# First steps of the convolution stage in another order: head 0's own work first, set-up inside head 0's steps

## The chip, the cores and the metric

One Trainium2 chip; the kernel runs on one of its cores. The metric is the time of one execution on the device in microseconds (us). An execution uses five instruction queues that run beside each other, each in its own order: PE (the matrix engine, TensorE), DVE (VectorE), ACT (ScalarE), POOL (GpSimd) and SP (which here only issues transfers). Semaphores let one wait for another.

## The reference

The kernel computes four blocks with residual sums: a long convolution between `x` and a context, a mixture-of-experts block, an attention block and a feed-forward block. Only the first one, and the preparation of the second that runs beside it, matter here:

```python
x = x + conv(layernorm(x), k, bias, ctx, ctx)      # first block
def conv(v, k, bias, x1, x2):                      # B=16, D=256, L=512, 8 rows to a head, 32 heads
    vr, x1r, x2r = (a.reshape(B, 32, 8, L) for a in (v, x1, x2))
    kv = vr[:, :, :, None, :] * x2r[:, :, None, :, :]
    y = causal_convolution(kv, k)                  # each head has one filter of 512 taps
    y = y + kv * bias.reshape(32, 8)[None, :, :, None, None]   # the skip term
    return einsum('bhijl,bhil->bhjl', y, x1r)
```

## The kernel before

`front_phase` is the first of three phases. It loops over 32 heads `h`; a head has two halves `u` and four steps `lb`. A half holds 4 product tiles of 128x512 (positions on the partitions). For each, `product` (POOL) multiplies the transposed rows `vt` with the turned context `ct` into `kf`. For the first two of a half, `parts` (ACT, `kh`) and `lows` (DVE for even, POOL for odd, `kl`) split it into a rounded part and a remainder. `conv` (PE) sums them against the filter's Toeplitz blocks: three matmuls per pair for `th`, `tl`, and one in full precision with their sum `t0` for the rest. A half takes 24 matmuls, 3 in its step 0, 9 up to its step 1, and the result of each step goes to one of four banks `Y`. DVE multiplies it with the context (`z`) and sums it (`R`).

Around this every head needs: `load` (SP: rows `x`, context `cr`, turned context `ct`, filter), `stats`, `shift` and `norm` (the layer norm: DVE, one exponentiation on POOL, DVE, ACT `xn`), `turn` (four PE transposes, an ACT copy to `vt`), `filt` and `filt_lo` (the filter through PE into `th`, `tl`, then `t0` on POOL), `weigh`, `skips` and `residual` (the skip term: DVE `w`, a PE matmul with the block of ones, DVE `sk`, POOL sum). The filters of heads 0 and 1 come straight from `k`; those of later heads from a table `kpad` in device memory that `split_filters` makes once: load `k`, round it (ACT, L108), residue (DVE, L109), store both (POOL, L293). `setup` (L419 on) loads what the next block needs, `gw`, `b1s`, `rb` and the bias table `f0b` (73x512), converts the last (ACT and DVE, `f_br`), and fills small constants on POOL. `clear` zeroes parts of a buffer `xs` from a tile of zeros. `shared_weights` takes one of eight 128x512 pieces of the shared weights: it converts the piece loaded one head before (ACT copy, POOL remainder, `c_sw`) and loads the next. `logit` and `best` handle the expert choice from head 2 on.

Each engine's queue is filled in the order in which the Python code calls these helpers. A wait is put down with the helper that needs it, so an engine that waits in one holds up everything queued behind it. In before, `load(0)`, `load(1)` and all of head 0's preparation, `split_filters` and `setup` are called ahead of the first `product`; in every head `shared_weights` and, from head 2 on, `logit` are called in half 0, step 1.

Of the kernel before, what the change touches and what calls it, by code (L numbers as in the profile page):

```python
# [126 lines left out]
def front_phase(nc, ctx, d, before, xa, idx, gat, ident, mhalf, n_heads=NHC):  # L127
# [110 lines left out]
    c_ob = p.do("gpsimd", lambda e: e.memset(ones_b, 1.0))  # L238

    v3 = ones_b.rearrange("p (b j) -> p b j", j=8)  # L240
    c_ob = p.do("gpsimd", lambda e: e.affine_select(out=v3, in_=v3, compare_op=ALU.is_ge, fill=0.0, base=0,
                                                    pattern=[[-8, 16], [0, 8]], channel_multiplier=1), c_ob)
    c_ob = p.do("gpsimd", lambda e: e.affine_select(out=v3, in_=v3, compare_op=ALU.is_ge, fill=0.0, base=7,
                                                    pattern=[[8, 16], [0, 8]], channel_multiplier=-1), c_ob)
    c_anr = p.do("vector", lambda e: e.tensor_copy(antir, anti), c_an)
    dsk = p.dsem("sk")
    c_sk = p.dma("sync", dsk, lambda e: e.dma_start(skip[:, :], d["skipt"]))
# [6 lines left out]
    c_z = p.do("gpsimd", lambda e: e.memset(zero[:, :], 0.0))  # L254
# [13 lines left out]
    def load(h):  # L268
        s = h % 2
        T["x", h] = p.dma("sync", dx[h % 4], lambda e: e.dma_start(xt[:, h % 4, :], d["x"][:, 8 * h:8 * h + 8, :]),  # L270
                          g("out", h - 4), gu("xb", h - 4))
        T["cr", h] = p.dma("sync", dr[s], lambda e: e.dma_start(cr[:, s, :], d["ctx"][:, 8 * h:8 * h + 8, :]),
                           g("sx", h - 2), g("w", h - 2))
        T["ct", h] = p.dma("sync", dc[h % 3], lambda e: e.dma_start(ct[:, h % 3, :, :], d["ctxh"][h]), g("z", h - 3), g("kv", h - 3))

        if h < 2:
            base = d["k"][h, 1:2]
            ap = bass.AP(base.tensor, base.offset, [[1, 128], [1, 512]])
            T["tf", h] = p.dma("sync", dt_[s], lambda e: e.dma_start(tf[:, s, :], ap))
# [28 lines left out]
    def filt_lo(h):  # L308
        s = h % 2
        if h < 2:  # L310
            T["tl", h] = p.do("vector", lambda e: e.tensor_tensor(tl[:, s, :], PT[:, :], f32(th[:, s, :]), ALU.subtract), g("th", h), g("mm", h - 2))
        else:
            T["pt", h] = p.do("tensor", lambda e: e.matmul(PT[:, :], antir, tr[:, s, 1, :], start=True, stop=True), g("tf", h), g("th", h))
            T["tl", h] = p.do("scalar", lambda e: e.activation(tl[:, s, :], PT[:, :], ACT.Copy), g("pt", h), g("mm", h - 2))
        T["t0", h] = p.do("gpsimd", lambda e: e.tensor_tensor(t0[:, s, :], f32(th[:, s, 0:256]), f32(tl[:, s, 0:256]), ALU.add), g("th", h), g("tl", h), g("mm", h - 2))
# [398 lines left out]
    stats(1)  # L714
    shift(1)
    split_filters()
    setup()
    units = [(h, u, mb) for h in range(n_heads) for u in range(2) for mb in range(4)]
    for n in range(4):
        product(*units[n])  # L720
        parts(*units[n])
    product(*units[4])
    for h in range(n_heads):
        more = h + 1 < n_heads
        for u in range(2):
            for lb in range(4):
# [11 lines left out]
                if u == 0 and lb == 0 and more:  # L738
                    weigh(h + 1)
# [1035 lines left out]
```

How the kernel before makes its waits and increments, by code:

```python
    def emit(self, e, eng):  # L72
        seen = {}
        def wait(sem, v):
            if seen.get(id(sem), 0) < v:
                eng.wait_ge(sem, v)
                seen[id(sem)] = v
        for sem, v in self.before:
            wait(sem, v)
        for fn, waits, inc in self.q[e]:
            for w in waits:
                if w is not None:
                    wait(*w)
            ins = fn(eng) if fn else None
            if inc:
                ins.then_inc(*inc)
# [1665 lines left out]
                def run(eng, e=e):  # L1754
                    for p in phases:
                        p.emit(e, eng)
                    if e == "sync":
                        for sem, v in before:
                            eng.wait_ge(sem, v)
```

## Time and profile before

| what | value |
|---|---|
| median of 3 executions | 3274.34 us (3273.34 to 3274.57) |
| profiled execution | 3277.38 us |
| its span, first to last instruction | 3275.6 us |
| PE busy over the span | 3175.7 us (97%) |
| DVE, ACT, POOL busy | 2173.6, 1267.7, 1051.4 us |
| PE's mean granted clock | 0.99 of full speed |
| instructions | 51687 |

The profile is one execution. Its busy times say how long each engine had an instruction running, an average over three quite different phases; the convolution stage is about the first 620 us. Records of PE overlap since matmuls are pipelined, so the distance between the starts tells the pace. Names begin with `c_` or `f_` for tiles of this phase; a number at the end is left out.

### The profile page before, as it was taken

The page shows a single profiled execution, that of the slowest core. Times are in us where ns is not written, and L with a number is a line of the kernel's source. Part 1 is how long each engine was busy: PE and PEld are TensorE (multiplying, and loading weights), DVE is VectorE, ACT ScalarE, POOL GpSimd, SP SyncE. Part 2 cuts the span into 40 slices and gives each one's busy share as a digit, 9 for nine tenths or more (in the row PEclk, how much of TensorE's full clock was granted, in tenths as well). Part 3 has the DMA queues.
Part 4 walks back from the last instruction along what each step waited for, and adds up shares of the span by engine and source line. Part 5 has one row for each costly group of instructions (what it writes and reads, how often), then busy time and mean ns, then how long its engine had stood idle before and what let it go on. Part 6 is the DMA issues. An engine that isn't in the chain of part 4 may idle for free.

```text
span 3275.6 us, 51687 instructions
## 1 busy us (share of the span) xinstructions
PE 3175.7 (97%) x18581; PEld 2699.7 (82%) x18581; DVE 2173.6 (66%) x5817; ACT 1267.7 (39%) x3058; POOL 1051.4 (32%) x1111
## 2 busy tenths in 40 slices
PE   7999999999999889999999999999998999999999
PEld 4666666689899769999999999999997788888887
DVE  6888888756555577778878787777776533333332
ACT  2333333333344345555555555555554311111111
POOL 7877777535211122222222222222201011010110
PEclk9999999999999899999999999999999999999999
DMA  4544443259644521111111111111101300000000
GB/s 129 155 142 133 132 140 95 81 171 313 194 155 151 207 90 53 46 46 46 46 46 40 39 46 46 46 39 40 46 14 44 108 26 26 26 26 26 26 14 13
DMA packets 123780, 267.41 MB, mean 82 GB/s; under 512 B 17689, under 2 KB 18337, under 8 KB 123530
## 3 DMA queue, kind: packets, MB, share of 16 engines
q1 hardware_dynamic: 100122, 186.59, 18.2%
q0 software_dynamic: 23408, 77.51, 7.0%
q8 instruction: 153, 2.51, 0.3%
q14 instruction: 97, 0.79, 0.1%
HBM read 159.49 MB, written 104.56 MB: 81 GB/s over the span
## 4 chain that ended last, share of the span: by engine, by line
PE 79%; DVE 9%; POOL 7%; ACT 1%; DMA 1%; issue 1%; SPq 0%; POOLq 0%; DVEq 0%
PE g_PH L1046 11%; PE g_O L1069 11%; PE t_U L1511 10%; PE t_S L1463 9%; PE t_PO L1498 5%; PE t_M L1447 5%; POOL c_kf L358 3%; PE t_T L1485 3%; PE f_Y L920 3%; PE f_Y L691 3%; PE t_M L1402 2%; PE f_Y L385 2%; PE f_Y L390 2%; DVE c_R L403 2%; DVE c_z L397 2%; PE t_M L1384 2%
## 5 line engine op out<-in xcount | busy, mean ns | idle before, releaser
L1473 ACT ACTIVATE t_pr<-t_sm,t_nb 128x256 f32<-128x256 f32 x512 | 256.5, 502 | 368.5 <-DVE t_nb L1469 368.5
L1059 DVE CAST g_hh<-g_hf 128x512 fp32r<-128x512 f32 x128 | 61.8, 483 | 434.7 <-PE g_O L1069 429.9
L1417 POOL TENSOR_TENSOR t_r<-t_r 128x256 f32<-128x256 f32 x128 | 95.9, 750 | 778.9 <-DVE t_rw L1479 451.7
L358 POOL TENSOR_TENSOR c_kf<-c_vt,c_ct 128x512 f32<-128x512 f32 x256 | 296.6, 1179 | 0.0
L1058 ACT ACTIVATE g_hf<-g_PH,g_b1s 128x512 f32<-128x512 f32 x128 | 88.2, 689 | 519.1 <-PE g_PH L1046 519.1
L1480 DVE TENSOR_SCALAR t_pr<-t_pr,t_rw 128x256 f32<-128x256 f32 x512 | 222.0, 434 | 18.2
L390 PE MATMUL f_Y<-c_kh,c_th 128*128 128x512 f32 x448 | 199.9, 446 | 9.6 <-ACT c_kh L365 9.6
L1046 PE MATMUL g_PH<-g_xh,g_w1h 128*128 128x512 f32 x512 | 205.3, 401 | 1.5 <-DVE g_xl L1034 1.5
L1046 PE MATMUL g_PH<-g_xh,g_w1l 128*128 128x512 f32 x512 | 203.0, 396 | 0.0
L1046 PE MATMUL g_PH<-g_xl,g_w1h 128*128 128x512 f32 x512 | 202.6, 396 | 0.0
L1069 PE MATMUL g_O<-g_w2h,g_hh 128*128 128x512 f32 x512 | 202.3, 395 | 0.0
L1069 PE MATMUL g_O<-g_w2h,g_hl 128*128 128x512 f32 x512 | 202.1, 395 | 0.0
L1511 PE MATMUL t_U<-t_voh,t_oth 128*128 128x512 f32 x512 | 201.7, 394 | 0.0
L1511 PE MATMUL t_U<-t_voh,t_otl 128*128 128x512 f32 x512 | 201.7, 394 | 0.0
L1069 PE MATMUL g_O<-g_w2l,g_hh 128*128 128x512 f32 x512 | 201.5, 394 | 0.0
L1469 DVE CUSTOM_DVE_ANT_0 t_sm<-t_S,t_mk 128x256 f32<-128x256 f32 x512 | 194.8, 418 | 9.6 <-PE t_S L1463 9.6
L1511 PE MATMUL t_U<-t_vol,t_oth 128*128 128x512 f32 x512 | 200.8, 392 | 0.0
L397 DVE TENSOR_TENSOR c_z<-f_Y,c_ct 128x512 f32<-128x512 f32 x256 | 174.1, 680 | 33.2 <-PE f_Y L385 32.9
L1490 DVE TENSOR_TENSOR t_ptl<-t_T,t_pth 128x512 fp32r<-128x512 f32 x256 | 175.6, 686 | 15.1 <-ACT t_pth L1489 15.0
L385 PE MATMUL f_Y<-c_kf,c_t 128*128 128x512 f32 x384 | 185.4, 591 | 0.0
L403 DVE TENSOR_REDUCE c_R<-c_z 128x64 f32<-128x512 f32 x256 | 174.9, 683 | 6.7
L390 PE MATMUL f_Y<-c_kl,c_th 128*128 128x512 f32 x448 | 177.8, 397 | 0.0
(356 smaller groups left out, 9696.1 us busy)
## 6 DMA issues: line engine op xcount, KB each, us to landing
xs<-c_zero SPq DMA_DIRECT2D x71, 256.0 KB, 5.2
f_xg<-xs SPq DMA_DIRECT2D x71, 256.0 KB, 2.8
ys<-f_yt POOLq DMA_DIRECT2D x71, 256.0 KB, 2.4
c_tr<-kpad SPq DMA_DIRECT2D x60, 256.0 KB, 4.8
f_xg<-xn SPq DMA_DIRECT2D x40, 256.0 KB, 4.6
c_xt<-x SPq DMA_DIRECT2D x32, 256.0 KB, 3.5
c_cr<-ctx SPq DMA_DIRECT2D x32, 256.0 KB, 3.9
c_ct<-ctxh SPq DMA_DIRECT2D x32, 256.0 KB, 4.4
```

What stands on the lines that cost most here:

```text
L358: T["kv", h] = T["kv1", n] = p.do("gpsimd", lambda e: e.tensor_tensor(o, iv, ic, ALU.mult), g("vt", h), g("ct", h), g("kl", n - 8), g("kh" ...
L385: last = p.do("tensor", lambda e, c=c, mb=mb: e.matmul(Y[y % 4][:, :], t0[:, s, c], kf[:, v, mb, :], start=False, stop=mb == lb), g("t0", ...
L390: last = p.do("tensor", lambda e, a=a, b_=b_, c=c, mb=mb, i=i: e.matmul(Y[y % 4][:, :], a[:, s, c], b_[:, v, mb, :], start=(mb == 0 and i ...
L397: T["z", h] = T["z1", y] = p.do("vector", lambda e: e.tensor_tensor(zz.rearrange("p (b j i) -> p b j i", i=8, j=8), iv, ic, ALU.mult), las ...
L403: T["red", y] = T["R", h] = p.do("vector", lambda e: e.tensor_reduce(rr, zr, AXX, ALU.add), g("z1", y), g("pr", h - 2))
L1046: T["ph", n] = p.do("tensor", lambda e, kk=kk, a=a, b_=b_, i=i: e.matmul(ph[:, :], a[:, k, kk, :], b_[:, s, kk, :], start=i == 0, stop=i = ...
L1069: tk = p.do("tensor", lambda e, a=a, b_=b_, t=t, fin=fin, c=c, beg=beg: e.matmul(O[t][:, :], a[:, n % 2, c], b_[:, k, :], start=beg, stop= ...
L1463: a = p.do("tensor", lambda e, t=t, j=j, q=q, k=k: e.matmul(PS1[:, 256 * t:256 * t + 256], q, k[:, s, :], start=j == 0, stop=j == 4), g("q ...
L1469: T["am", N] = am = p.do("vector", lambda e, t=t, k4=k4: e.tensor_tensor_reduce(out=sm[:, k4, :], in0=PS1[:, 256 * t:256 * t + 256], in1=m ...
L1473: T["ex", x] = p.do("scalar", lambda e, t=t, k4=k4: e.activation(pr[:, N % 2, t, :], sm[:, k4, :], ACT.Exp, bias=nb[:, k4, 0:1], scale=-1. ...
L1480: T["nm", x] = p.do("vector", lambda e, t=t, k4=k4: e.tensor_scalar(pr[:, N % 2, t, :], pr[:, N % 2, t, :], rw[:, k4, 1:2], None, ALU.mult ...
L1511: a = p.do("tensor", lambda e, t=t, tt=tt, j=j, o=o, w=w: e.matmul(PU[t][:, :], o[:, N % 3, tt], w[:, h, :], start=h == 0 and j == 0, stop ...
```

## The change

Three things are done. First, `load` is cut into four parts, and head 0's rows, filter and turned context are issued ahead of the rest; head 0's normalisation, transposes, filter and its first product follow directly, and product 1 comes after the statistics of head 1. Second, what is left of the preparation moves between head 0's steps: `split_filters` and the block of ones behind step 0, the skip term and the tile of zeros behind step 1, its residual sum behind step 2 and `setup` behind step 3; the skip product of head 1 moves from step 0 to step 2. Third, `shared_weights` is called in half 1, step 0 of every head instead of half 0, step 1.

```diff
-    c_ob = p.do("gpsimd", lambda e: e.memset(ones_b, 1.0))
...
-    c_sk = p.dma("sync", dsk, lambda e: e.dma_start(skip[:, :], d["skipt"]))
...
-    c_z = p.do("gpsimd", lambda e: e.memset(zero[:, :], 0.0))
...
+    def block_ones():
+
+        c_ob = p.do("gpsimd", lambda e: e.memset(ones_b, 1.0))
...
+        U["ones",] = c_ob
...
+        if h:
+            sum_filter(h)
+
+    def sum_filter(h):
+        s = h % 2
         T["t0", h] = p.do("gpsimd", lambda e: e.tensor_tensor(t0[:, s, :], f32(th[:, s, 0:256]), f32(tl[:, s, 0:256]), ALU.add), g("th", h), g("tl", h), g("mm", h - 2))
...
-    load(0)
-    load(1)
+    load_rows(0)
+    load_filter(0)
+    load_turned(0)
+    load_rows(1)
+    load_context(0)
+    U["skip",] = p.dma("sync", dsk, lambda e: e.dma_start(skip[:, :], d["skipt"]))
+    load_turned(1)
+    load_context(1)
+    load_filter(1)
     stats(0)
+    shift(0)
+    norm(0)
+    turn(0)
     filt(0)
     filt_lo(0)
-    shift(0)
-    norm(0)
-    weigh(0)
-    turn(0)
-    skips(0)
-    residual(0)
+    units = [(h, u, mb) for h in range(n_heads) for u in range(2) for mb in range(4)]
+    product(*units[0])
+    parts(*units[0])
+    sum_filter(0)
     stats(1)
     shift(1)
-    split_filters()
-    setup()
-    units = [(h, u, mb) for h in range(n_heads) for u in range(2) for mb in range(4)]
-    for n in range(4):
+    for n in range(1, 4):
         product(*units[n])
         parts(*units[n])
     product(*units[4])
...
-                if u == 0 and lb == 0 and more:
+                if u == 0 and lb == (0 if h else 2) and more:
                     weigh(h + 1)
...
                 conv(h, u, lb, units[n] if n < len(units) and lb == 0 else None)
                 if u == 0 and lb == 3 and h:
                     finish(h - 1)
+                if h == 0 and u == 0:
+                    if lb == 0:
+                        split_filters()
+                        block_ones()
+                    if lb == 1:
+                        weigh(0)
+                        skips(0)
+                        U["zero",] = p.do("gpsimd", lambda e: e.memset(zero[:, :], 0.0))
+                    if lb == 2:
+                        residual(0)
+                    if lb == 3:
+                        setup()
...
-                if u == 0 and lb == 1:
+                if u == 1 and lb == 0:
                     shared_weights()
-                    if h > 1:
-                        logit(h - 2)
+                if u == 0 and lb == 1 and h > 1:
+                    logit(h - 2)
```

POOL's queue from head 0's exponentiation (`c_rs`) on, before:

```order
L123 TENSOR_TENSOR c_rs<-c_rs,mhalf 128x1 [waits c_vector]
L315 TENSOR_TENSOR c_t<-c_th,c_tl 128x256 [waits c_vector,c_scalar]
L349 TENSOR_TENSOR c_sk<-c_sk,c_xt 128x512 [waits c_x0,c_vector]
L123 TENSOR_TENSOR c_rs<-c_rs,mhalf 128x1 [waits c_vector]
L293 DMA kpad<-f_xh 32x640 [waits c_vector,c_scalar]
L293 DMA kpad<-f_xl 32x640
L428 MEMSET f_gt 128x146
L430 MEMSET f_gt 128x2 [waits c_gpsimd]
L430 MEMSET f_gt 128x2 x2
L431 MEMSET c_onef 128x128
L433 AFFINE_SELECT c_trif<-c_onef 128x128 [waits c_gpsimd]
L436 IOTA c_iota 128x8
```

And in the changed kernel, from the same place:

```order
L123 TENSOR_TENSOR c_rs<-c_rs,mhalf 128x1 [waits c_vector]
L378 TENSOR_TENSOR c_kf<-c_vt,c_ct 128x512 [waits c_c0,c_scalar]
L335 TENSOR_TENSOR c_t<-c_th,c_tl 128x256 [waits c_vector,c_scalar]
L123 TENSOR_TENSOR c_rs<-c_rs,mhalf 128x1 [waits c_vector]
L378 TENSOR_TENSOR c_kf<-c_vt,c_ct 128x512
L393 TENSOR_TENSOR c_kl<-c_kf,c_kh 128x512 [waits c_gpsimd,c_scalar]
L378 TENSOR_TENSOR c_kf<-c_vt,c_ct 128x512 x4
L308 DMA kpad<-f_xh 32x640 [waits c_vector,c_scalar]
L308 DMA kpad<-f_xl 32x640
L292 MEMSET c_ones_b 128x128
L295 AFFINE_SELECT c_ones_b<-c_ones_b 128x128 [waits c_gpsimd]
L297 AFFINE_SELECT c_ones_b<-c_ones_b 128x128 [waits c_gpsimd]
```

The two stores of the filter table and the block of ones (`c_ones_b`, which stood ahead of all this) now come behind six products, and the small fills of `setup` have left this place.

SP's queue from head 1's filter on, before:

```order
L279 DMA f_xg<-k 128x512
L289 DMA f_xg<-k 32x640
L421 DMA c_gw<-gw 128x32
L422 DMA f_b1s<-sb 128x4
L423 DMA c_rb<-rb 8x256
L424 DMA f_stg<-f0b 73x512
L447 DMA f_stg<-sw 128x512
L270 DMA c_xt<-x 128x1x512
L272 DMA c_cr<-ctx 128x1x512 [waits c_vector]
L274 DMA c_ct<-ctxh 128x512
L284 DMA c_tr<-kpad 128x512 [waits c_tensor,c_ko]
L284 DMA c_tr<-kpad 128x512
```

And in the changed kernel:

```order
L259 DMA c_xt<-x 128x1x512
L264 DMA c_cr<-ctx 128x1x512 [waits c_vector]
L268 DMA c_ct<-ctxh 128x512
L280 DMA c_tr<-kpad 128x512 [waits c_tensor,c_ko]
L280 DMA c_tr<-kpad 128x512
L252 DMA xs<-c_zero 128x512 [waits c_gpsimd]
L252 DMA xs<-c_zero 128x512 x2
L441 DMA c_gw<-gw 128x32
L442 DMA f_b1s<-sb 128x4
L443 DMA c_rb<-rb 8x256
L444 DMA f_stg<-f0b 73x512
L467 DMA f_stg<-sw 128x512
```

The four loads of `setup` (`gw`, `sb`, `rb`, `f0b`) stood ahead of head 2's rows; they now stand behind head 2's context, which waits for DVE (`c_vector`, the skip term of head 0), behind the filter loads from `kpad` and behind three clears.

ACT's queue from the first product's rounded part on, before (its first row is the table's rounding):

```order
L108 ACTIVATE f_xh<-f_xg 32x640 [waits c_kp]
L426 ACTIVATE f_br<-f_stg 73x512 [waits c_uc0]
L365 ACTIVATE c_kh<-c_kf 128x512 [waits c_gpsimd] x2
L323 ACTIVATE c_xn<-c_xt,c_nm,c_rs 128x512 [waits c_x1,c_vector]
L365 ACTIVATE c_kh<-c_kf 128x512 [waits c_gpsimd] x2
L337 ACTIVATE c_vt<-f_PV 128x512 [waits c_tensor]
L306 ACTIVATE c_th<-f_PT 128x512 [waits c_tensor]
L365 ACTIVATE c_kh<-c_kf 128x512 [waits c_gpsimd] x2
```

And in the changed kernel:

```order
L385 ACTIVATE c_kh<-c_kf 128x512 [waits c_gpsimd] x2
L343 ACTIVATE c_xn<-c_xt,c_nm,c_rs 128x512 [waits c_x1,c_vector]
L385 ACTIVATE c_kh<-c_kf 128x512 [waits c_gpsimd]
L108 ACTIVATE f_xh<-f_xg 32x640 [waits c_kp]
L385 ACTIVATE c_kh<-c_kf 128x512 [waits c_gpsimd]
L357 ACTIVATE c_vt<-f_PV 128x512 [waits c_tensor]
L446 ACTIVATE f_br<-f_stg 73x512 [waits c_uc0]
L321 ACTIVATE c_th<-f_PT 128x512 [waits c_tensor]
L385 ACTIVATE c_kh<-c_kf 128x512 [waits c_gpsimd] x2
```

The conversion of the bias table (`f_br`, which waits for the transfers `c_uc0`) stood ahead of all copies of products; it now stands ahead of head 1's filter copy `c_th` and of the copies of head 1's first two products.

## Rows read from the trace of the kernel before

**Rows 1.** windows: time, length, then busy us (instructions) per engine, PE clock, DMA share, GB/s

```profile
16.00:17.00 1.00, 0.46 (x1) 0.00 (x0) 0.50 (x1) 0.00 (x0) 0.00 (x0) 1.00 0.06 25
26.00:30.00 4.00, 3.90 (x10) 3.11 (x11) 1.76 (x2) 0.77 (x2) 3.85 (x4) 1.00 1.03 335
61.97:81.42 19.45, 18.51 (x79) 12.91 (x78) 16.67 (x32) 6.91 (x12) 15.90 (x16) 1.00 0.52 149
238.27:257.22 18.95, 18.67 (x79) 12.91 (x78) 16.62 (x33) 6.28 (x11) 14.66 (x15) 1.00 0.44 140
```

**Rows 2.** timeline of PE: start us, us, engine, line, op, names; in brackets the idle time before

```profile
26.10 0.77 PE L390 MATMUL f_Y<-c_kh,c_th 128*128 128x512 f32 x1 [9.64 <-ACT c_kh L365]
...
44.52 0.79 PE L390 MATMUL f_Y<-c_kh,c_th 128*128 128x512 f32 x1
```

**Rows 3.** chain that ended last, 0 to 60 us: start us, us, what

```profile
12.67 0.82 ACT c_xn L323
...
13.54 1.12 PE f_PV L335 x4
14.65 1.82 PE f_PSK L342 x2
...
19.22 0.80 DVE f_xl L109
...
20.63 1.22 POOL kpad L293 x2
...
23.34 2.08 POOL c_kf L358 x2
...
32.78 1.40 PE f_Y L390 x6
```

**Rows 4.** timeline of POOL in the first 34 us

```profile
2.38 0.41 POOL L241 TENSOR_SCALAR_AFFINE_SELECT c_ones_b<-c_ones_b 128x128 f32<-128x128 f32 x1
...
5.92 0.56 POOL L123 TENSOR_TENSOR c_rs<-c_rs,mhalf 128x1 f32<-128x1 f32 x1 [2.19 <-DVE c_rs L122]
...
26.14 1.28 POOL L373 TENSOR_TENSOR c_kl<-c_kf,c_kh 128x512 fp32r<-128x512 f32 x1 [0.74 <-ACT c_kh L365]
27.38 6.08 POOL L358 TENSOR_TENSOR c_kf<-c_vt,c_ct 128x512 f32<-128x512 f32 x5
```

**Rows 5.** timeline of ACT (ScalarE), 0 to 82 us

```profile
11.19 0.60 ACT L306 ACTIVATE c_th<-f_PT 128x512 fp32r<-128x512 f32 x1 [9.10 <-PE f_PT L303]
...
18.98 0.63 ACT L426 ACTIVATE f_br<-f_stg 73x512 fp32r<-73x512 f32 x1 [3.08 <-DMA f_stg<-f0b]
...
30.98 0.63 ACT L365 ACTIVATE c_kh<-c_kf 128x512 fp32r<-128x512 f32 x1 [4.21 <-POOL c_kf L358]
...
68.56 0.16 ACT L499 ACTIVATE c_lg<-f_PV 128x8 f32<-128x8 f32 x1
```

**Rows 6.** timeline of SP's DMA issues, 0 to 30 us

```profile
6.68 0.47 SPq L421 DMA_DIRECT2D c_gw<-gw  x1
...
8.22 0.24 SPq L424 DMA_DIRECT2D f_stg<-f0b  x1
...
17.21 0.54 SPq L272 DMA_DIRECT2D c_cr<-ctx  x1
...
23.41 0.81 SPq L284 DMA_DIRECT2D c_tr<-kpad  x2
24.26 1.45 SPq L262 DMA_DIRECT2D xs<-c_zero  x3
```

**Rows 7.** timeline of DVE, 26 to 48 us

```profile
37.49 0.69 DVE L397 TENSOR_TENSOR c_z<-f_Y,c_ct 128x512 f32<-128x512 f32 x1
...
41.78 0.69 DVE L120 BATCH_NORM_STATS2 c_st<-c_xt 128x6 f32<-128x512 f32 x1
...
42.79 0.68 DVE L311 TENSOR_TENSOR c_tl<-f_PT,c_th 128x512 fp32r<-128x512 f32 x1
```

**Rows 8.** source line L262, the three clears at 24 to 26 us

```profile
DMA to landing us min/median/max: 4.3/4.5/5.0
```

More of the change, by code:

```diff
@@ L261, in clear @@
         for c in left[:n]:
-            U["clr",] = p.dma("sync", dz, lambda e, c=c: e.dma_start(xsz[:, c:c + 512], zero[:, :]), c_z)
+            U["clr",] = p.dma("sync", dz, lambda e, c=c: e.dma_start(xsz[:, c:c + 512], zero[:, :]), U["zero",])
         del left[:n]
@@ L266, in g, with load_rows, load_context, load_turned @@
         return T.get(k)
-    def load(h):
-        s = h % 2
+    def load_rows(h):
         T["x", h] = p.dma("sync", dx[h % 4], lambda e: e.dma_start(xt[:, h % 4, :], d["x"][:, 8 * h:8 * h + 8, :]),
                           g("out", h - 4), gu("xb", h - 4))
+    def load_context(h):
+        s = h % 2
         T["cr", h] = p.dma("sync", dr[s], lambda e: e.dma_start(cr[:, s, :], d["ctx"][:, 8 * h:8 * h + 8, :]),
                            g("sx", h - 2), g("w", h - 2))
+    def load_turned(h):
         T["ct", h] = p.dma("sync", dc[h % 3], lambda e: e.dma_start(ct[:, h % 3, :, :], d["ctxh"][h]), g("z", h - 3), g("kv", h - 3))
+    def load_filter(h):
+        s = h % 2
         if h < 2:
@@ L284, in load @@
                 T["tf", h] = p.dma("sync", dt_[s], lambda e, q=q, ap=ap: e.dma_start(f32(tr[:, s, q, :]), ap), T["kp",], g("pt", h - 2))
+    def load(h):
+        load_rows(h)
+        load_context(h)
+        load_turned(h)
+        load_filter(h)
+    dsk = p.dsem("sk")
+    def block_ones():
+        c_ob = p.do("gpsimd", lambda e: e.memset(ones_b, 1.0))
+        v3 = ones_b.rearrange("p (b j) -> p b j", j=8)
+        c_ob = p.do("gpsimd", lambda e: e.affine_select(out=v3, in_=v3, compare_op=ALU.is_ge, fill=0.0, base=0,
+                                                        pattern=[[-8, 16], [0, 8]], channel_multiplier=1), c_ob)
+        c_ob = p.do("gpsimd", lambda e: e.affine_select(out=v3, in_=v3, compare_op=ALU.is_ge, fill=0.0, base=7,
+                                                        pattern=[[8, 16], [0, 8]], channel_multiplier=-1), c_ob)
+        U["ones",] = c_ob
     def split_filters():
@@ L314, in filt_lo @@
             T["tl", h] = p.do("scalar", lambda e: e.activation(tl[:, s, :], PT[:, :], ACT.Copy), g("pt", h), g("mm", h - 2))
+        if h:
+            sum_filter(h)
+    def sum_filter(h):
+        s = h % 2
         T["t0", h] = p.do("gpsimd", lambda e: e.tensor_tensor(t0[:, s, :], f32(th[:, s, 0:256]), f32(tl[:, s, 0:256]), ALU.add), g("th", h), g("tl", h), g("mm", h - 2))
@@ L329, in weigh @@
                                                                    in1=cr[:, s, :], op0=ALU.mult, op1=ALU.mult),
-                         g("xn", h), c_sk, g("cr", h), g("psk", h - 2))
+                         g("xn", h), U["skip",], g("cr", h), g("psk", h - 2))
     def turn(h):
@@ L342, in skips @@
         T["psk", h] = p.do("tensor", lambda e: e.matmul(PSK[:, :], ones_b, w[:, s, :], start=True, stop=True),
-                           c_ob, g("w", h), g("sx", h - 1))
+                           U["ones",], g("w", h), g("sx", h - 1))
         a = p.do("vector", lambda e: e.tensor_tensor(sk[:, s, :], cr[:, s, :], PSK[:, :], ALU.mult), g("psk", h), g("out2", h - 2))
```

6 lines of the change are left out of this document (removed).

## The prediction

> **What bounds the kernel now.** I read the windows first, then the chain that ended last, then the timelines of the engines over the first 48 us. The windows of two whole heads [rows 1] show a period of 19.45 us in an early head and 18.95 us in a later one, with PE busy for more than 17.7 of them in both, DVE for 16.6 and POOL for 14.7 to 15.9: this stage runs at the pace of PE with DVE close behind, and POOL has slack. So nothing that only moves work off POOL is worth anything in mid-stage. What counts is when the regular rhythm starts, and what the two periods differ by. The rhythm starts late: PE sits idle for 9.64 us before the first convolution matmul at 26.10 [rows 2]. The chain before it [rows 3] is the whole set-up in a row: normalise 12.67, transposes 13.54, the skip term's matmul 14.65, the filter table's residue 19.22, its two stores 20.63, and only then the first products at 23.34. The reader is to see that little of this feeds a convolution, so that there is something to win. The question is where the displaced work queues up.
>
> **The part that gets earlier.** Head 0's exponentiation on POOL stood at 5.92 [rows 4]. The rows' load moves up one issue, worth the 0.47 to 0.54 us that an issue takes [rows 6]: I take 0.45, which gives 5.5 to 6.0, the normalised rows at 6.3, transposes at 7.2 and their copy at 8.3 (0.87 and 1.15 later, as 12.67, 13.54 and that one's 1.12 [rows 3]). The first product runs from 9.0 to 10.0 (2.08 for two [rows 3]). The filter's matmul queues on PE behind the transposes: 8.3 to 10.4, its copy to 11.0 (0.60 [rows 5]), its residue to 11.7 (0.68 [rows 7]). POOL's second exponentiation now stands ahead of product 1. It waits for DVE's statistics of head 1, which stand behind the filter residue and the first low part: 12.6, 1.0 us of statistics (41.78 to 42.79 [rows 7]), 0.4 of hand-overs and 0.56 on POOL: 14.5. Product 1 ends at 15.6; the low part starts 0.7 later and takes 1.28 [rows 4]: 17.6, against 27.4 before. **This is a lead of 9.8 us, and the first convolution is ready at 12.7.**
>
> **Where the lead goes.** On PE the skip matmul now stands right behind the second convolution step, and it needs the block of ones. On POOL these three instructions stand behind four products and the two stores of the filter table, and the stores wait for DVE's residue, behind low part 4. Product 4 to its copy: 27.38 to 30.98 is 3.6 [rows 4, 5], so 21.2. Copy 0.63, low part and a reduction 1.5 (0.68 to 0.88 for such a DVE instruction), residue 0.80 [rows 3]: 24.1. The stores begin 0.6 after it and take 1.22 [rows 3]: 25.9. The ones: longest of three 0.41 [rows 4], I take 1.2 together: 27.2. The skip matmul there lasts 2.0 (14.65 to 16.5 and a start [rows 3]), the second convolution step having ended long ago: 29.2. In before PE stood at this very step, nine matmuls on, near 29.9: from 26 to 30 only ten ran, so 0.43 us apart after 26.10, and later six in 1.40 us, 0.23 each [rows 1 to 3]. After its new pause from about 20 to 27 PE runs so slowly again, 3.4 more matmuls at 0.2 us each, and the lead of 0.7 is used up: it ends the third step at 32.2 as before. (A slow start of this kind, nine matmuls at 0.2 more, costs 1.7 us; after a pause of 7 us rather than 9.6 it is assumed, so 0 to 1.7.) **Value of the earlier start for PE: 0 (bounds: 0, and the 9.8 if PE never waited).**
>
> A rule says why those matmuls are slow. The Trainium skill (TensorE: Matmul & The Clock Gate, "Part 1: The HAM clock gate") says that an idle PE falls back to half its clock and is released by activity. The spacing of 0.43 and 0.23 agrees, the granted clock of 1.00, the 2.4 GHz level, in the window of 26 to 30 [rows 1] does not. By the rule every restart after such a pause is slow, by the granted clock none is; the two differ by those 1.7 us.
>
> **The part that gets later.** This decides it. SP's second row load waits for the skip term's DVE product: 17.21 before [rows 6], now 29.2 + 0.7 = 29.9. Behind it on SP stand, in this order, the turned context, two filter loads, three clears, and then set-up's four loads, which in before were issued from 6.68 to 8.22. From 17.21 the first two take 1.2, the filter loads 0.85, the clears 1.5, the three small ones 1.54 [rows 6]: the bias load (f0b) is issued at 35.05 instead of 8.22. The third clear (issued near 33) lands 4.3 to 5.0 after issue [rows 8], at 37.3 to 38.5, the longer with two more 256 KB loads ahead. The bias load is odd: 73 partitions, 146 KB. In the window 16 to 17 the queue carries 25 GB/s at a DMA share of 0.06, one sixteenth [rows 1], with nothing else pending, and ACT waits 3.08 us until 18.98 for exactly this load [rows 5]. I read this as one of 16 engines carrying it alone: 149.5 kB at 25 GB/s is 6.0 us. So it lands at 43.3 to 44.5; I take 43.7.
>
> That reading has a rule behind it. The Trainium skill (DMA: Bandwidth & Descriptors, "Why a DMA increments its semaphore by 16 and not by 1") says that a transfer goes over the largest number of engines up to 16 that divides its slowest dimension; 73 is prime, so one. The trickle agrees.
>
> On ACT the conversion of this load (f_br) now stands behind head 0's transposed copy and **ahead of head 1's filter copy** and of the copies of products 8 and 9. All wait until 43.75. On DVE the residue of f_br and three small casts stand ahead of z4: 0.4 after ACT starts, 0.68 and some 0.7 for the casts: z4 at 45.6 to 45.8, 37.49 before. From z4 to head 1's filter residue 5.30 us passed [rows 7], of which some 0.2 was waiting: that residue starts at 50.9 instead of 42.79, **8.1 us late**. POOL's filter sum and head 1's first convolution wait for it. PE runs on through its eighth step to about 44.6 (it has four output banks), then waits to 51.6 for head 1's first matmul, which began at 44.52 before [rows 2]: 7.1 late, and 8.8 if it restarts slowly. DVE and POOL are 8.1 late and pace head 1 as much as PE does. **I take 8.4 (bounds 7.1 and 8.8 for this landing time; 5.5 to 10 with it).**
>
> **The shared weights.** Their conversion moves from step 1 to step 4 of each head. At its old place ACT does it between product 9's copy and the logit copy: the logit copy comes at 68.56 [rows 5], and PE's transposes behind it wait for the bank. The two windows [rows 1] differ in just this pair, ACT 6.91 against 6.28 busy and POOL 15.90 against 14.66, and by 0.50 to 0.52 us in length. Heads 2 to 8 have both a logit and a conversion: 7 x 0.51 = 3.6 us. At the new place POOL comes to the exponentiation, where it waits for DVE (2.19 us even in head 0 [rows 4]), and it has 18.95 - 14.66 = 4.3 us idle in a later head, ACT 12.7 [rows 1]; so the 1.2 us are hidden there and count 0. If that cover is gone it costs what it did, 3.6. **Term: -3.6 (bounds -3.6 and 0.)**
>
> Set-up's POOL work (1.4 us), the zero fill and the residual sum move into head 0's steps. POOL has then not caught up on its old place and is still 1 to 2 us ahead, and later waits for the filter sum anyway: 0. The filter loads of head 2 come 8 us later and are used half a head after head 1 begins, which is itself late: 0.
>
> **Sum:** 0 + 8.4 - 3.6 = +4.8 us. The profiled execution of before took 3277.38 (span 3275.6, 1.8 around it), 3.0 above the median of 3274.34; it would give 3282.2, and the median 3279.1.
>
> **Rivals.**
> - *The bias load is no straggler, or lands ahead of the clears.* For it: it is small. Against: the 25 GB/s. It would land 4.5 us after its issue, as the clears do [rows 8]: ACT is free at 39.6, 4.1 earlier, so 8.4 becomes 4.3, sum +0.7: 3275.0. Chance 0.17. If it stalls nobody, -3.6: 3270.7, chance 0.08.
> - *The shared conversion costs the same at its new place* (ACT would do it between the copies of products 12 and 13). For it: ACT is in order and product 13's copy comes 0.5 later. Against: that copy is needed a step later. Sum +8.4, 3282.7: slower by 0.26%. It decides from 1.8 us of the 3.6 lost. Chance 0.15.
> - *The lead is kept*: the ones and the bias load turn out early and POOL's 9.8 us carry through. For it: the rows of start-up. Against: the order of POOL and SP. -9.8 - 3.6: 3260.9, the one case that is faster. Chance 0.05.
> - *The change does nothing*: excluded as a mechanism, since the order differs, but 3275 is close to it.
>
> **How the numbers follow.** The forecast has 0.55, its own range 3276 to 3281. A measurement of this kernel tells about 0.2%, 6.5 us, from no change, so the forecast and the first rival in both its forms count as no change: 0.80; slower 0.15, faster 0.05. The range reaches to the case without a stall and to the one with the conversion's price: 3270.7 to 3282.8. It leaves out the kept lead and what lies above.
>
> **What would show it.** In the profile after: the first product near 9, the first convolution matmul near 12.7; PE idle from about 20 to 27 and again from 44.6 to 51.6; ACT waiting some 10 us before f_br for f_stg<-f0b, until 43.7; head 1's filter residue at 50.9 and its sum on POOL near 51.7; and 18.95 between the filter sums of heads 3 to 9. It is wrong if f_br starts before 40, or if the periods stay at 19.45.

## The result and the profile after

Before and after were timed on one chip in turn: 3274.77 us before (3273.34 to 3280.19, 6 runs) and 3285.61 us after (3284.84 to 3287.93, 6 runs), a ratio of 1.003 with a 95% interval of 1.002 to 1.0041. The change makes the kernel 0.3% slower, 10.8 us by the medians. The forecast of 3279.1 was too low, and the result lies 2.8 us above the range. The profiled execution took 3286.95 us (span 3285.2), 9.6 more than that of before.

The loss can be placed to some tenths of a microsecond by a beacon, an instruction that runs once a period: here POOL's filter sum (`c_t`), once a head. First the timeline of POOL before, then after, the rows of the sums of heads 1, 2, 9 and 31:

```profile
43.55 0.73 POOL L315 TENSOR_TENSOR c_t<-c_th,c_tl 128x256 f32<-128x256 f32 x1
61.97 0.73 POOL L315 TENSOR_TENSOR c_t<-c_th,c_tl 128x256 f32<-128x256 f32 x1
...
198.23 0.73 POOL L315 TENSOR_TENSOR c_t<-c_th,c_tl 128x256 f32<-128x256 f32 x1
...
620.73 0.72 POOL L315 TENSOR_TENSOR c_t<-c_th,c_tl 128x256 f32<-128x256 f32 x1
```

```profile
45.77 1.26 POOL L393 TENSOR_TENSOR c_kl<-c_kf,c_kh 128x512 fp32r<-128x512 f32 x1 [8.67 <-ACT c_kh L385]
...
51.78 0.73 POOL L335 TENSOR_TENSOR c_t<-c_th,c_tl 128x256 f32<-128x256 f32 x1
72.14 0.74 POOL L335 TENSOR_TENSOR c_t<-c_th,c_tl 128x256 f32<-128x256 f32 x1
...
123.89 1.27 POOL L488 TENSOR_TENSOR c_sw<-f_stg,c_sw 128x512 fp32r<-128x512 f32 x1 [1.22 <-ACT c_sw L487]
...
209.34 0.74 POOL L335 TENSOR_TENSOR c_t<-c_th,c_tl 128x256 f32<-128x256 f32 x1
...
631.87 0.73 POOL L335 TENSOR_TENSOR c_t<-c_th,c_tl 128x256 f32<-128x256 f32 x1
```

The sum of head 1 is 8.23 us late, that of head 2 is 10.17 late, that of head 9 is 11.11 late, and that of head 31 is 11.14 late. So the whole loss arises in three places: 8.23 in start-up, 1.94 in head 1, and 0.94 in the seven periods from the sum of head 2 to that of head 9. The period, the distance of one head's sum from the next, was 19.47 there and is 19.60; from the sum of head 9 on both kernels have the same distances within 0.03, 18.95 in most heads. What follows the last sum takes 2654.9 us of the span before and 2653.3 after, and it scatters by a few us from one execution to the next: beacons compare parts, and medians compare kernels.

Start-up, in the chain that ended last of the kernel after (start, length, what):

```profile
25.33 0.41 POOL c_ones_b L297
...
32.21 1.30 SPq L441
33.55 1.09 SPq L442
...
34.68 0.38 SPq L443
...
35.11 8.41 DMA f_stg<-f0b
43.54 0.64 ACT f_br L446
44.20 0.68 DVE f_br L447
...
45.36 0.59 DVE c_z L417
45.95 1.63 DVE c_kl L393
...
51.10 0.61 DVE c_tl L326
...
51.80 6.45 PE f_Y L410 x15
```

The longest piece before head 1 is the bias load: issued at 35.11 instead of 8.22 [rows 6], it takes 8.41 us, and what follows in the chain, up to head 1's first matmul, starts from its landing. `c_tl`, the filter residue, is the last thing that this matmul waits for. On PE, the timeline shows the two pauses and what comes behind the second:

```profile
25.79 2.08 PE L362 MATMUL f_PSK<-c_w,c_ones_b 128*128 128x512 f32 x2 [7.28 <-POOL c_ones_b L297]
...
51.80 0.77 PE L410 MATMUL f_Y<-c_kh,c_th 128*128 128x512 f32 x1 [7.69 <-DVE c_tl L326]
52.36 0.63 PE L410 MATMUL f_Y<-c_kh,c_tl 128*128 128x512 f32 x1
52.79 0.63 PE L410 MATMUL f_Y<-c_kl,c_th 128*128 128x512 f32 x1
...
59.62 0.40 PE L410 MATMUL f_Y<-c_kh,c_tl 128*128 128x512 f32 x1
59.85 0.40 PE L410 MATMUL f_Y<-c_kl,c_th 128*128 128x512 f32 x1
```

```profile
50.00:52.00 2.00, 0.20 (x1) 0.23 (x2) 1.93 (x6) 0.00 (x0) 0.79 (x2) 0.50 0.27 42
52.00:54.00 2.00, 2.00 (x5) 1.59 (x6) 1.93 (x5) 0.82 (x1) 2.00 (x3) 0.50 0.27 97
54.00:56.00 2.00, 2.00 (x6) 1.54 (x5) 1.93 (x3) 0.00 (x0) 2.00 (x2) 0.50 0.46 145
56.00:58.00 2.00, 2.00 (x6) 1.57 (x6) 1.04 (x2) 1.26 (x2) 2.00 (x3) 0.56 0.84 154
58.00:62.00 4.00, 4.00 (x17) 2.51 (x16) 3.00 (x5) 0.60 (x1) 4.00 (x4) 1.00 0.72 248
```

The second fence holds windows of the kernel after, with the granted clock (the share of full speed that TensorE was allowed) third from the end. Behind the pause of 7.69 us matmuls start 0.43 apart at a granted clock of 0.50 (the 1.2 GHz level) and then 0.23 apart at 1.00 (2.4 GHz). The chain has 6.45 us for head 1's first fifteen.

The last place is mid-stage. The timeline of DVE, the low part of a filter product in head 4 and in head 12:

```profile
124.37 1.33 DVE L393 TENSOR_TENSOR c_kl<-c_kf,c_kh 128x512 fp32r<-128x512 f32 x1
...
281.35 0.68 DVE L393 TENSOR_TENSOR c_kl<-c_kf,c_kh 128x512 fp32r<-128x512 f32 x1
```

The same instruction takes 1.33 us in an early head and 0.68 in a later one. The early one overlaps the shared weights' remainder on POOL (`c_sw` at 123.89, above), which the change has put there. A second pair like it shows in start-up: POOL's low part at 45.77 (above) and DVE's at 45.95, which takes 1.63 in the chain.

### The profile page after: what moved, and what is told of

Read it like the earlier page. It is cut to its first block, busy times and chain, and to the rows that moved or that the text cites. A ratio compares the mean times of both kernels' runs of the same rounds, so it can differ in the third digit from the quotient of the medians.

```text
span 3285.2 us, 51684 instructions
## 1 busy us (share of the span) xinstructions
PE 3178.4 (97%) x18581; PEld 2700.9 (82%) x18581; DVE 2182.1 (66%) x5817; ACT 1267.4 (39%) x3058; POOL 1052.2 (32%) x1111
## 4 chain that ended last, share of the span: by engine, by line
PE 78%; DVE 10%; POOL 7%; ACT 1%; DMA 1%; issue 1%; SPq 0%; POOLq 0%; DVEq 0%
PE g_PH L1083 11%; PE g_O L1106 11%; PE t_U L1548 10%; PE t_S L1500 9%; PE t_PO L1535 5%; PE t_M L1484 5%; POOL c_kf L378 3%; PE t_T L1522 3%; PE f_Y L957 3%; PE f_Y L711 3%; PE t_M L1439 2%; DVE c_R L423 2%; PE f_Y L405 2%; PE f_Y L410 2%; DVE c_z L417 2%; PE t_M L1421 2%
```

## The experiments

All were timed in turn with the kernel before on their chip. The last three columns hold beacons: the filter sums of heads 1 and 2, the mean period from head 2 to head 9, and the sum of head 31. Two theories stood at the start: that the late bias load sets head 1 (A), and that POOL's remainder of the shared weights slows DVE's low part (D). Rivals were that something else late in start-up holds head 1 back, and that the conversion on ACT costs at its new place what it did at its old.

| run | median us (runs) | before, same chip | ratio, 95% | sums of heads 1, 2 | period | last sum |
|---|---|---|---|---|---|---|
| e1_loads_early | 3277.48 (11) | 3275.66 | 1.0008 [0.9999, 1.0017] | 44.95, 63.58 | 19.60 | 623.38 |
| e2_bias_split | 3279.14 (11) | 3275.66 | 1.0011 [1.0002, 1.002] | 46.92, 65.54 | 19.60 | 625.20 |
| e3_shared_old_place | 3282.97 (11) | 3275.66 | 1.0023 [1.0014, 1.0032] | 52.20, 70.85 | 19.47 | 629.66 |
| e4_before_logit_first | 3272.46 (11) | 3275.66 | 0.9991 [0.9982, 1.0] | 43.83, 62.19 | 18.95 | 617.40 |
| e5_ones_early | 3282.61 (10) | 3278.55 | 1.0013 [1.0004, 1.0022] | 47.14, 65.75 | 19.60 | 625.47 |
| e7_no_remainder | 3282.14 (10) | 3278.55 | 1.0011 [1.0001, 1.002] | 51.53, 70.22 | 18.95 | 625.54 |
| e8_loads_logit | 3276.9 (11) | 3278.55 | 0.999 [0.9981, 0.9999] | 44.28, 62.62 | 18.95 | 617.77 |
| e9_skip_late | 3275.67 (11) | 3278.55 | 0.9991 [0.9982, 1.0] | 45.14, 63.50 | 18.95 | 618.82 |
| e10_pe_awake | 3293.62 (5) | 3278.23 | 1.0045 [1.0032, 1.0059] | 52.10, 77.40 | 19.60 | 637.12 |
| e11_pe_awake_short | 3287.69 (8) | 3276.97 | 1.003 [1.0019, 1.004] | 51.39, 70.02 | 19.60 | 629.81 |

The beacon and the medians agree: the last sum's distance from 620.73 and the difference of the medians lie within 1.7 us of each other in every row. For e1 they are +2.7 and +1.8, for e4 -3.3 and -3.2, for e10 +16.4 and +15.4.

**e1_loads_early**: the changed kernel with set-up's four loads issued in head 0's first step.

```diff
-    def setup():
+    def setup_loads():
 
         p.dma("sync", dc0, lambda e: e.dma_start(gw[:, :, :], d["gw"]))
...
         nst[0] = 1
+
+    def setup():
+
...
                     if lb == 0:
                         split_filters()
+                        setup_loads()
                         block_ones()
```

> The changed kernel, but set-up's four loads are issued right behind the load of the filter table, in head 0's step 0; its arithmetic stays in step 3. Theory A (the bias load, late on SP and carried by one of 16 engines, holds up ACT and all of head 1): the conversion f_br follows head 0's copy at about 32.5, head 1's filter residue comes near 41.5 instead of 51.0, PE does not pause at 42.7, and the kernel gains 9 to 12 us on the changed one, to about 3275. Rival B (the start-up is late because of the skip matmul's wait for the block of ones, 18.1 to 25.8, and what POOL does behind it): nothing of that is touched, so under 2 us gained.

The last sum moves from 631.87 to 623.38, a gain of 8.49 us: a little under the 9 to 12 of theory A, and far from rival B's 2. PE's pause ahead of head 1 is gone; the rest of start-up stays. PE, and DVE's part:

```profile
44.98 0.47 PE L410 MATMUL f_Y<-c_kh,c_th 128*128 128x512 f32 x1 [0.39 <-issue]
```

```profile
36.87 1.25 DVE L450 TENSOR_TENSOR f_br<-f_stg,f_br 9x512 fp32r<-9x512 f32 x1
38.15 1.20 DVE L455 CAST c_one<-c_onef 128x128 fp32r<-128x128 f32 x1
...
44.20 0.68 DVE L326 TENSOR_TENSOR c_tl<-f_PT,c_th 128x512 fp32r<-128x512 f32 x1
```

Head 1's filter residue starts at 44.20, 2.7 later than expected: the conversion's residue and the first cast take 1.25 and 1.20, while they take 0.68 and 0.23 in the chain of after where POOL stands still. They run here beside POOL's products and its low part. These 1.54 us are about what is left of the delay: head 1's sum, at 44.95, is 1.40 later than in before.

**e2_bias_split**: the changed kernel with the bias load in two pieces; nothing is issued earlier.

```diff
-        U["c0",] = p.dma("sync", dc0, lambda e: e.dma_start(stg[0:73, 0, :], d["f0b2"]))
+        p.dma("sync", dc0, lambda e: e.dma_start(stg[0:64, 0, :], d["f0b2"][0:64]))
+        U["c0",] = p.dma("sync", dc0, lambda e: e.dma_start(stg[64:73, 0, :], d["f0b2"][64:73]))
```

> The changed kernel, but the 73-partition bias load is two loads, of 64 and of 9 partitions, at the same place. Theory A (one engine carries 73 partitions): both land about 4.5 us after their issue, f_br begins near 39.5 to 40 instead of 43.54, and everything from head 1 on is 3.5 to 4 us earlier; a gain of about 4 us. Rival C (the load is late only because of what is queued ahead of it, not because of its shape): f_br stays at 43 to 44 and the time at the changed kernel's.

The timeline of ACT:

```profile
38.67 0.63 ACT L447 ACTIVATE f_br<-f_stg 73x512 fp32r<-73x512 f32 x1 [5.59 <-DMA f_stg<-f0b]
```

The conversion starts 4.87 us earlier than the 43.54 of after, more than the 3.5 to 4 expected, the filter sum of head 1 is 4.86 earlier and the last sum 6.67. (The further 1.8 arise in head 1: PE's pause is only 2.18 us here, its granted clock stays at 1.00, and the sums of heads 1 and 2 lie 18.62 apart.) That shows two things: it is the shape of this load that makes it slow, since the bytes and the place in the queue are the same, and start-up hangs on it one for one. The Trainium skill (DMA: Bandwidth & Descriptors, "Why a DMA increments its semaphore by 16 and not by 1") has a load go over the largest number of engines up to sixteen that divides its slowest dimension: one for 73 partitions, sixteen for 64, nine for 9. For the 73 partitions the trace of after agrees: while nothing else is under way, its window shows 26 GB/s at a DMA share of 0.07, about one sixteenth.

```profile
39.00:43.00 4.00, 4.00 (x15) 2.64 (x14) 0.00 (x0) 0.00 (x0) 0.00 (x0) 1.00 0.07 26
```

How many engines carried the 64 and the 9 no run here shows; the 4.87 us fit.

**e3_shared_old_place** and **e4_before_logit_first** ask what the shared weights cost at either place.

```diff
e3, on the changed kernel:
-                if u == 1 and lb == 0:
+                if (u == 0 and lb == 1) if h else (u == 1 and lb == 0):
                     shared_weights()
e4, on the kernel before:
                 if u == 0 and lb == 1:
-                    shared_weights()
                     if h > 1:
                         logit(h - 2)
+                    shared_weights()
```

> The changed kernel, but the shared weights are converted in half 0, step 1 again (from head 1 on). Theory D (at the new place POOL's remainder runs beside DVE's low part, which then takes 1.33 instead of 0.68 us on the path, while at the old place ACT's copy delays the logit copy by 0.5): the distance between filter sums of heads 2 to 8 goes from 19.60 to 19.46, the low part of step 4 takes 0.68 again, about 1 us gained over seven heads and up to 0.7 in head 1. Rival E (the conversion is hidden at the new place and the periods are long for another reason of the new order): no change of the periods.

> The kernel before, with logit called ahead of shared_weights in half 0, step 1, nothing else. Theory D: ACT's logit copy no longer waits behind the 0.6 us conversion, and POOL's remainder stays where it runs beside DVE instructions that read PSUM; the periods of heads 2 to 8 fall from 19.46 to about 18.95, 3.6 us gained on before, near 3271. Rival E: POOL's 1.27 us cost something wherever they are and the periods stay above 19.3, under 1 us gained.

In e3, at the old place, the period is 19.47, as before, and DVE's low part takes 0.68 again; head 1 gains more than the 0.7 expected, 1.71 (18.65 for 20.36), which comes up again below. In e4, with the logit's copy ahead of the conversion, the period is 18.95. So the 0.51 per head was indeed the logit's copy waiting for the conversion on ACT, and the 3.6 us of the prediction are there to be had: e4 has its last sum 3.33 earlier than before. What the conversion costs at the new place they leave open.

**e7_no_remainder**: the changed kernel, with POOL's subtraction for the shared weights replaced by a memset of its result; it leaves out the low parts of the shared expert's weights.

```diff
-            U[key] = U["wl", i] = p.do("gpsimd", lambda e: e.tensor_tensor(to[1], src, f32(to[0]), ALU.subtract), U["wh", i], U["wd", i])
+            U[key] = U["wl", i] = p.do("gpsimd", lambda e: e.memset(f32(to[1]), 0.0), U["wh", i], U["wd", i])
```

> The changed kernel, but POOL's remainder of the shared weights is a fill with zeros instead of a subtraction with two operands (so the shared expert's result lacks its low parts). Theory D (the subtraction beside DVE's low part slows that one down): the low part of step 4 takes 0.68 instead of 1.33 us, the distance of the filter sums of heads 2 to 8 falls from 19.60 to 18.95, and the stage ends 4.5 to 5.5 us earlier than the changed kernel's. Rival H (ACT's copy, which delays product 13's copy, or the loads cost it): the periods stay at 19.5 or above.

POOL, then DVE, in head 4:

```profile
120.66 0.53 POOL L488 MEMSET c_sw<- 128x512 f32 x1 [1.20 <-ACT c_sw L487]
```

```profile
121.16 0.68 DVE L393 TENSOR_TENSOR c_kl<-c_kf,c_kh 128x512 fp32r<-128x512 f32 x1
```

The memset has all but ended when DVE's low part starts; this takes 0.68, and the period is 18.95. ACT's conversion is untouched. POOL's own length is not what counts: behind the subtraction of after it is idle for 2.22 us, until DVE hands it its next input. This isolates the cause: 0.65 us in each early head is DVE's low part waiting for POOL's subtraction. The last sum is 6.33 us earlier, more than the 4.5 to 5.5 expected, since head 1 is shorter too, by 1.67 (18.69 for 20.36). The Trainium skill (SBUF — State Buffer, "🔬 SBUF: two separate sides") says that a VectorE instruction in a two-port mode, or with two SBUF inputs beside a GpSimd one that reads SBUF, and the GpSimd instruction exclude each other for the whole instruction. The trace agrees: POOL's ends at 125.16 (123.89 and 1.27), and DVE's ends 0.54 later, at 125.70, as if it had begun only then. In e1 both slow instructions look alike: POOL's products end at 37.58 and DVE's residue at 38.12, POOL's low part ends at 39.27 and the cast at 39.35.

**e10_pe_awake** and **e11_pe_awake_short** ask what PE's slow restart has to do with head 1's 1.94 us: spare matmuls on PE in its pause, 60 and 23 of them (the cut shows e11).

```diff
+                if h == 1 and u == 0 and lb == 0:
+                    for _ in range(23):
+                        p.do("tensor", lambda e: e.matmul(Y[0][:, 0:128], ident, ident, start=True, stop=True), c_id, g("z1", 4), inc=False)
                 conv(h, u, lb, units[n] if n < len(units) and lb == 0 else None)
```

> The changed kernel with sixty spare 128 x 128 matmuls (identity by identity, 0.11 us each by the four transposes in 0.44 us, so some 6.6 us) put ahead of head 1's first convolution matmul on TensorE, into a bank that this matmul starts afresh. Nothing else is moved, and the bias load still holds head 1 back to a filter sum at 51.8. Theory that TensorE's slow restart after its pause is worth 1.7 us: the granted clock from 50 to 58 is 1.00, head 1's matmuls start 0.23 apart and not 0.43, the filter sums of heads 1 and 2 lie 18.6 us apart and not 20.36, the last filter sum is at 630.1 +- 0.3 and not at 631.87, and the time is about 3284 us. Rival, that VectorE and the shared weights' remainder set head 2's filter sum anyway: the matmuls are faster, the distance stays at 20.3 and the last filter sum at 631.9. Third: the clock falls or the restart is slow all the same, since the matmuls behind the pause are of another kind: spacing 0.43 and distance 20.3.

> As the run before it, with 23 spare matmuls in place of sixty: a float matmul of this size is two records of 0.112 us (13.66 us for 120), so 23 take 5.2 us, from 46.3, where their bank comes free, to 51.5. TensorE then pauses for 1.9 us and not for 7.7 ahead of them, and they are done when head 1's filter is. Theory that the slow restart is worth 1.7 us: granted clock 1.00 from 50 to 58, head 1's matmuls 0.23 apart from about 51.8, the filter sums of heads 1 and 2 18.6 apart and not 20.36, the last filter sum at 630.1, the time about 3284 us. Rival, that VectorE and the shared weights' remainder set head 2's filter sum anyway: the matmuls 0.23 apart, the distance 20.3, the last filter sum at 631.9 and the time as that of the changed kernel.

Sixty were too many: a float matmul of this size shows as two records, so they ran for 13.66 us, to 60.0, and held head 1's convolution back. The run says nothing on the distance of 20.36 (its own is 25.30), but head 1's matmuls started 0.23 apart right behind them. With 23 the pause is covered. Windows and PE's timeline of e11:

```profile
52.00:54.00 2.00, 2.00 (x10) 1.64 (x9) 1.97 (x5) 0.82 (x1) 2.00 (x3) 1.00 0.06 20
54.00:56.00 2.00, 2.00 (x9) 1.24 (x9) 1.55 (x3) 0.09 (x1) 2.00 (x3) 1.00 0.80 227
```

```profile
45.62 5.40 PE L776 MATMUL f_Y<-ident 128*128 128x128 f32 x46 [1.37 <-DVE c_z L417]
51.41 0.47 PE L410 MATMUL f_Y<-c_kh,c_th 128*128 128x512 f32 x1 [0.39 <-issue]
51.72 0.39 PE L410 MATMUL f_Y<-c_kh,c_tl 128*128 128x512 f32 x1
```

The granted clock stays at 1.00, the matmuls are 0.23 apart, and the filter sums of heads 1 and 2 lie 18.63 apart instead of 20.36, 1.73 less. (The last sum is 2.06 earlier; 0.39 of it is there at the sum of head 1 already.) The median does not resolve these 2 us: its ratio is 1.003, like that of the changed kernel.

Yet 1.73 is not the price of a slow restart alone. In e3 and e7 PE pauses for 8.63 and 8.30 us, the granted clock behind the pause is 0.50 and the matmuls start 0.43 apart, and still the two sums lie only 18.65 and 18.69 apart, where before has 18.42. What these two lack is POOL's subtraction in step 4 of head 1. From the chain of after, the chain of e3, and DVE's timeline of e11:

```profile
65.30 1.59 DVE c_kl L393
```

```profile
52.23 5.73 PE f_Y L410 x15
...
65.02 0.60 DVE c_kl L393
```

```profile
63.12 1.65 DVE L393 TENSOR_TENSOR c_kl<-c_kf,c_kh 128x512 fp32r<-128x512 f32 x1
```

After loses 0.72 us against e3 in head 1's first fifteen matmuls (6.45 and 5.73: thirteen starts were slow there, ten here) and 0.99 in the low part (1.59 and 0.60). Together that is 1.71, the whole difference between 20.36 and 18.65. In e11 the low part is as slow as in after, but PE is on time and the distance is 18.63. So two things make up the 1.94 us, a slow PE and a low part held up by POOL. Without the slow PE 0.21 are left (e11); without the subtraction, and with ten slow starts, 0.23 (e3) and 0.27 (e7). Why thirteen starts were slow in one kernel and ten in the two others, and what thirteen would cost without the subtraction, no run shows.

**e5_ones_early** and **e9_skip_late** ask why PE's earlier start brings nothing; the theory was that the ones stand too far back in POOL's queue (F). e5 is e1 with the block of ones made at the start. e9 is e8 (below: e1 with the logit ahead of the shared weights) with the ones and the zero tile made at the start, head 0's skip term one step later, and head 2's loads one step later.

```diff
e5:
+    block_ones()
     load_rows(0)
...
-                        block_ones()
e9, besides (parts):
+    U["zero",] = p.do("gpsimd", lambda e: e.memset(zero[:, :], 0.0))
...
-                if u == 0 and lb == 2 and h + 2 < n_heads:
+                if u == 0 and lb == (2 if h else 3) and h + 2 < n_heads:
...
                     if lb == 1:
                         weigh(0)
-                        skips(0)
-                        U["zero",] = p.do("gpsimd", lambda e: e.memset(zero[:, :], 0.0))
                     if lb == 2:
-                        residual(0)
+                        skips(0)
                     if lb == 3:
+                        residual(0)
                         setup()
```

> As e1 (set-up's loads early), and the block of ones is made at the start, where POOL idles from 2.2 to 5.6. Theory F (the skip matmul waits for the ones alone, and this eats the lead of 9.8 us): PE's pause before it shrinks from 7.3 to about 2 us and head 1 starts 4 or 5 us earlier than in e1. Rival G (the skip product on DVE, queued behind the filter residue and the second step's sum, is ready only 1.1 us before the ones): the pause shrinks by 1.1 us to about 6.2 and the last filter sum comes about 1 us earlier than e1's 623.38.

> As e8, with the ones and the tile of zeros made at the start, and the skip term moved one step further back: its matmul behind step 2, its residual sum behind step 3, head 2's loads at step 3. Theory F or G, whichever delays the skip matmul: PE no longer pauses there from 18.7 to 26 but goes on with step 2, and part of the lead survives: head 1 begins 3 to 7 us earlier than in e8, the last filter sum near 613 to 616, time 3267 to 3270. Rival I (the lead is lost to POOL anyway, whose stores wait for DVE and delay products 6 and 7): head 1 begins within 1.5 us of e8.

Neither gains anything: against e1, e5's last sum is 2.09 later, where both theories had it earlier; against e8, e9's is 1.05 later and its head 1 sum 0.86, which is within the 1.5 of rival I. In e5 PE waits longer for the skip term, 11.14 us instead of 7.28, and now for DVE. PE, DVE and POOL of e5:

```profile
28.80 2.07 PE L362 MATMUL f_PSK<-c_w,c_ones_b 128*128 128x512 f32 x2 [11.14 <-DVE c_w L348]
```

```profile
23.78 4.97 DVE L348 SCALAR_TENSOR_TENSOR c_w<-c_xn,c_skip,c_cr 128x512 f32<-128x512 f32 x1
...
31.52 0.74 DVE L348 SCALAR_TENSOR_TENSOR c_w<-c_xn,c_skip,c_cr 128x512 f32<-128x512 f32 x1
```

```profile
24.42 1.08 POOL L378 TENSOR_TENSOR c_kf<-c_vt,c_ct 128x512 f32<-128x512 f32 x1
25.45 1.26 POOL L393 TENSOR_TENSOR c_kl<-c_kf,c_kh 128x512 fp32r<-128x512 f32 x1
26.65 0.53 POOL L788 MEMSET c_zero<- 128x512 f32 x1
27.13 1.06 POOL L378 TENSOR_TENSOR c_kf<-c_vt,c_ct 128x512 f32<-128x512 f32 x1
```

The skip term's product on DVE takes 4.97 us where it takes 0.74 with POOL at rest, and 0.74 in the kernel after, where the ones follow the filter stores: POOL, freed of the ones, runs four instructions without a gap, and DVE's ends 0.56 after the last of them (27.13 and 1.06, then 28.75). In e9, where POOL runs a product, a subtraction and a product there and no memset, two such products take 5.17 together and PE waits 6.38 for them. In after DVE's product ran from 23.96 to 24.70, beside POOL's last store and the start of the ones, and POOL's next product came only at 25.70; in e5 it comes at 24.42. So where the ones are not in the way, the lead is lost because DVE waits for POOL. That the ones had been the gap in which DVE got through follows from these times; no run tests it alone.

**e8_loads_logit** puts e1 and e4's order together on the changed kernel, from head 1 on.

> The two repairs together: set-up's loads early (e1), and the shared weights back in half 0, step 1, behind the logit (as e4). If the two costs are independent, the last filter sum comes at 623.38 - 7 x 0.65 = 618.8 and another 0.3 earlier for head 1, which is 1 to 2 us behind e4's 617.40; time about 3273, on a par with before or slightly under. If they share a bottleneck, less is gained over e1.

Its last sum is 617.77, where 618.5 was expected, and its ratio 0.999: with e9 the only version of the changed order that is no slower than before. It is no faster than e4 (0.9991), which leaves start-up as it was.

## Why the prediction was wrong

**Start-up: right.** First product at 9 (9.12), first convolution matmul at 12.7 (12.21), PE idle from about 20 to 27 (18.5 to 25.79), bias load issued at 35.05 (35.11), conversion at 43.7 (43.54), filter residue of head 1 at 50.9 (51.01), its sum near 51.7 (51.78). The sum's delay was put at 8.1 and is 8.23. e1 and e2 show that the bias load is its cause. The value of PE's earlier start was taken as 0, and it was 0: 0.98 us of it are left at PE's last step of head 0 (42.23 for 43.21), and PE waits them away. But the reason given for the lead's loss, the ones behind POOL's queue, is half of it. e5 and e9 show that DVE's skip product was late without them.

**The term of +8.4 us, the part that gets later, was too small: it measured 10.17** at the second filter sum, above its bounds of 7.1 and 8.8. The prediction let PE lose only what DVE and POOL did not lose anyway, with a slow restart as the upper bound. For a slow restart of ten matmuls by itself that is nearly borne out: in e3 and e7 it adds 0.23 and 0.27 to the delay of the sum. The step that failed is the bound, "8.8 if it restarts slowly". It has nothing behind the restart that could cost more than before. But in the same head POOL's subtraction now lies over DVE's low part, and in the chain the slow matmuls (51.80) and the slow low part (65.30) stand one behind the other; together they cost 1.94 and not some 0.2. The start was also slow for thirteen matmuls and not for nine.

**The term of -3.6 us, the shared weights, was the step that failed most: over the seven periods from head 2 to head 9 it measured +0.94.** It stood on POOL's 4.3 us and ACT's 12.7 us of idle time at the new place: "so the 1.2 us are hidden there and count 0". POOL's time is hidden, and ACT's too; the logit no longer waits, and those 3.6 us are real (e4, e7). But the POOL instruction was moved under DVE's low part, on the engine that paces the stage, and 0.65 us per head came back (e7). The prediction asked whether the moved instruction's own engine had room, and never which instruction of another engine it would overlap, though its own working has two durations, 0.68 and 0.88, for low parts on DVE. The timeline of before even has a third, beside POOL's products:

```profile
38.10 1.25 DVE L373 TENSOR_TENSOR c_kl<-c_kf,c_kh 128x512 fp32r<-128x512 f32 x1
```

The rival that kept the old price came nearest with 3282.7, but by another mechanism: it had ACT's copy cost the time, and e7 keeps that copy and has 18.95.

The sum by measured terms is 8.23 + 1.94 + 0.94 = 11.11 us, where +4.8 was forecast: 1.8 too little for the late part and 4.5 for the shared weights. By medians it is 10.8. The chance of 0.80 for no measurable change was too high: the upper bounds of both terms left out that one engine's work can slow another's. That start-up's delay came out at 8.23 for 8.1 is partly luck, for two misses cancel: DVE's product z4 began at 45.27 and not at 45.6 to 45.8, and its low part behind it took 1.71 us, where before had 1.25.

## What to carry to other kernels

Before an instruction is moved into an engine's idle time, look at what the neighbour engine runs in that place: here a POOL instruction that reads SBUF made a DVE one with two SBUF operands wait for 0.65 us, and since DVE is on the chain there, work hidden in POOL's idle time had its price back. The load of 73 partitions held up nothing on the chain near the head of the queue and was a straggler of 8.4 us behind others; follow each moved DMA to its landing and to what stands behind its reader. Follow a beacon through both traces: it splits a difference of 0.3% into places, which totals cannot. And before a price is put on one of two causes, take away each in turn: here e11 without the one and e3 without the other both lose 1.7 of the 1.94 us.

## What the runs showed of the hardware

- DVE's instructions with two operands in SBUF were held up beside POOL: the low part took 0.68 alone and 1.25 (before) to 1.73 (e2) beside POOL's work; the skip product 0.74 alone and 4.97 beside four POOL instructions without a gap (e5). It went the other way too: POOL's residual sum took 1.72 in after, where DVE's skip product ended inside it, and 1.26 in before. DVE instructions that read PSUM, and reductions, kept their 0.68 beside the same neighbours: the product at 123.78, just before the slow low part, took 0.67. The four in e5 include a memset, and DVE did not get through there either; whether a memset alone holds it up was not tried.
- A cast with a single input in SBUF was held up as well: 1.20 beside POOL's low part, 0.23 without (e1 and after).
- The granted clock was 0.50 after PE's pauses of 7.69, 8.63 and 8.30 us (after, e3, e7) and stayed at 1.00 when the pause was 1.37 or 2.18 us (e11, e2). In start-up it is no guide: behind PE's pause there, matmuls start 0.43 apart in after and in e11, while the window from 28 to 30 us shows 1.00 in after and 0.50 in e11. The prediction's doubt, whether matmuls 0.43 apart at a clock of 1.00 [rows 1] are slow, is answered by the spacing.
- The load of 73 partitions took 8.41 us from issue to landing; as 64 and 9 partitions the conversion behind it started 4.87 us sooner.
